# One fixed total of 832 GpSimd scatters, divided anew over the stages of an eight-stage graph network

## The reference

```python
edge_index = jnp.stack([src, dst])
x = x + _L0_gnn_ref(_layernorm(x), ..., src, dst)            # mean of neighbours
x = x + _L0_ffn_ref(_layernorm(x)[None], ...)[0]             # half of the nodes through an FFN
x = x + _L1_gnn_ref(_layernorm(x), ..., edge_attr_3, edge_index)   # attention over edges
x = x + _L1_ffn_ref(_layernorm(x)[None], ...)[0]             # 8 experts, top 1, capacity
x = x + _L2_gnn_ref(_layernorm(x), src, dst, edge_weight, ...)     # weighted sum over edges
x = x + _L2_ffn_ref(_layernorm(x)[None], ...)[0]             # 8 experts, top 2
x = x + _L3_gnn_ref(_layernorm(x), ..., edge_index)          # two GCN convolutions
x = x + _L3_ffn_ref(_layernorm(x)[None], ...)[0]             # 8 experts, top 1

def _L2_gnn_ref(x, edge_row, edge_col, edge_val, weight_l, bias_l, weight_r, bias_r):
    h = x @ weight_l
    agg = jax.ops.segment_sum(edge_val[:, None] * h[edge_col], edge_row, num_segments=N)
    return agg + bias_l + x @ weight_r + bias_r
```

## Time and profile before

| | us |
|---|---|
| median of 3 runs, without the profiler | 3591.89 |
| lowest and highest of these | 3591.84, 3598.81 |
| span of the profiled execution | 4271.3 |
| PE busy in it | 3169.9 |
| the 416 weight scatters, POOL busy | 463.5 |
| the 416 count scatters, POOL busy | 408.1 |

### The profile page before, as it was taken

How to read it: one execution, slowest core, us unless ns; L and a number is a source line. 1 busy time by engine, 2 the same in 40 slices (tenths; PEclk the granted TensorE clock), 3 DMA queues, 4 the chain that set the end, 5 groups by cost and what they waited for, 6 DMA issues and landing times. The chain is left out here.

```text
span 4271.3 us, 47439 instructions
## 1 busy us (share of the span) xinstructions
PE 3169.9 (74%) x14365; PEld 2194.5 (51%) x14365; DVE 1967.2 (46%) x4724; ACT 1137.9 (27%) x2521; POOL 2014.5 (47%) x2031
## 2 busy tenths in 40 slices
PE   4777777976888888459955886228975885998966
PEld 3565655854444445248843553114553553445856
DVE  5444446924666666899961342000024336023332
ACT  3444441221222222249931110000022221012310
POOL 5666664664555555675555553770035552000032
PEclk9888988987888988669977998558987997999978
DMA  5455452004766766248831225004313114452434
GB/s 176 159 160 160 160 159 94 1 13 142 197 198 192 202 186 199 68 151 271 281 117 63 93 65 197 23 15 136 128 45 128 52 52 141 151 198 86 152 125 137
DMA packets 281656, 563.05 MB, mean 132 GB/s; under 512 B 61793, under 2 KB 184101, under 8 KB 280774
## 3 DMA queue, kind: packets, MB, share of 16 engines
q1 hardware_dynamic: 200070, 404.27, 28.4%
q0 software_dynamic: 81344, 155.76, 13.4%
HBM read 381.99 MB, written 177.86 MB: 131 GB/s over the span
## 5 line engine op out<-in xcount | busy, mean ns | idle before, releaser
L1282 PE MATMUL bank<-layer_gnn_h_nodes,layer_gnn_s_onehot_t 128*128 x1664 | 547.9, 457 | 110.4 <-issue 73.5
L146 POOL DMA_INDIRECT edge_counts<-repeats,count_cell x416 | 408.1, 981 | 360.8 <-SPq L2872 226.5
L155 POOL DMA_INDIRECT edge_weights<-shares,share_cell x416 | 463.5, 1114 | 240.8 <-issue 91.9
L1234 POOL DMA_INDIRECT layer_gnn_s_rows<-gat_rows,src_cols x416 | 401.6, 965 | 355.2 <-DMA kept_rows<-layer_gnn_s_rows 211.3
L527 POOL DMA_INDIRECT layer_gnn_sum_rows<-xn_rows,src_cols x416 | 417.8, 1004 | 199.1 <-issue 110.8
L2841 PE MATMUL bank<-layer_gnn_b_weights,xn_nodes 128*128 128x391 f32 x768 | 300.7, 534 | 205.1 <-issue 173.3
L1282 PEld LDWEIGHTS bank<-layer_gnn_h_nodes,layer_gnn_s_onehot_t 128*128 128x128 f32 x1664 | 317.7, 212 | 208.8 <-issue 135.8
L2841 PEld LDWEIGHTS bank<-layer_gnn_b_weights,xn_nodes 128*128 128x128 f32 x768 | 155.5, 203 | 349.8 <-issue 225.1
L1292 ACT ACTIVATE layer_gnn_s_enc<-bank 128x256 f32<-128x256 f32 x416 | 154.7, 384 | 592.1 <-PE bank L1275 345.7
L590 PE MATMUL bank<-layer_gnn_sum_onehot,layer_gnn_sum_rows 128*128 128x256 f32 x832 | 296.8, 442 | 2.0 <-issue 1.8
L1311 DVE TENSOR_TENSOR layer_gnn_s_mix<-bank,layer_gnn_s_enc 128x256 f32<-128x256 f32 x416 | 176.0, 423 | 257.9 <-PE bank L1282 124.2
(11 more groups left out here) (645 smaller groups left out, 6077.7 us busy)
## 6 DMA issues: line engine op xcount, KB each, us to landing
kept_rows<-layer_gnn_s_rows SPq DMA_DIRECT2D x104, 512.0 KB
layer_gnn_w_rows<-kept_rows SPq DMA_DIRECT2D x104, 512.0 KB
edge_weights<-layer_gnn_sum_zeros SPq DMA_DIRECT2D x56, 800.0 KB
layer_gnn_gcn_sum_counts<-edge_counts SPq DMA_DIRECT2D x50, 896.0 KB
layer_gnn_b_weights<-edge_weights SPq DMA_DIRECT2D x56, 782.0 KB
layer_gnn_s_dst_across<-in_dst_row SPq DMA_DIRECT2D x104, 256.0 KB
edge_counts<-layer_gnn_w_no_edges SPq DMA_DIRECT2D x25, 896.0 KB
layer_ffn_e_w<-in_l1f_w SPq DMA_DIRECT2D x16, 1024.0 KB
```

The costliest lines, as they stand in the source:

```text
L146: nc.gpsimd.indirect_dma_start(g.counts, bass.IndirectOffsetOnAxis(ap=g.cell[:, t:t + 1].bitcast(U32), axis=0), g.repeats[:, t:t + 1], Non ...
L155: nc.gpsimd.indirect_dma_start(g.weights, bass.IndirectOffsetOnAxis(ap=g.share_cell[:, t:t + 1].bitcast(U32), axis=0), g.shares[:, t:t + 1 ...
L1234: nc.gpsimd.indirect_dma_start(rows[:, t % U, :], None, htable, bass.IndirectOffsetOnAxis(ap=g.srcc[:, t:t + 1].bitcast(U32), axis=0)).the ...
L1282: last = nc.tensor.matmul(g.ps[4 + t % 4][:, 0:D + HEADS], onehot_t[:, t % 4, k, :], hflat[:, ds(w * AW + (k * AW + HEADS), D + HEADS)], s ...
```

## The change

The two tables get other boundaries, `COUNTED` one entry more, and the count scatters of `weighted_products` a wait before each.

| stage | before | after |
|---|---|---|
| first FFN | 20 + 118 weights | the same |
| `gat_features` | 36 weights | 48 weights |
| `edge_softmax` | 36 weights | 50 weights |
| `weighted_sum`, on `summed` | 148 weights | 162 weights |
| gate of the second FFN | 16 weights | 18 weights |
| its route | 16 weights | 16 counts |
| its experts 0 and 1 | 13 weights + 12 counts each | 15, 16 counts |
| its experts 2 to 7 | 12, 12, 12, 12, 12, 13 counts | 15, 16, 15, 16, 15, 16 counts |
| `weighted_products` | 205 counts in one run | 162 counts, each behind a wait on `used` |
| all later stages | 114 counts | the same |

```diff
+def place_counts_beside(nc, g, pool, lo, hi, signal, first, steps):
+
+    for t in range(lo, hi):
+        pool.wait_ge(signal, first + (t - lo) * steps // (hi - lo))
+        place_counts(nc, g, pool, t, t + 1)
...
-PLACED = (20, 138, 174, 210, 358, 374, 390)
-COUNTED = (97, 302, 336, 348, 374)
+PLACED = (20, 138, 186, 236, 398, 416)
+COUNTED = (16, 140, 302, 336, 348, 374)
...
-        route(nc, g, "sw_route", logits, 1, CAP, SLOTS, r, g.xn, table, lambda pool: place_weights(nc, g, pool, PLACED[5], PLACED[6]))
+        route(nc, g, "sw_route", logits, 1, CAP, SLOTS, r, g.xn, table, lambda pool: place_counts(nc, g, pool, 0, COUNTED[0]))
...
-                first_of = lambda e: COUNTED[0] * e // E
-                left_of = lambda e: PLACED[6] + (ET - PLACED[6]) * min(e, 2) // 2
+                first_of = lambda e: COUNTED[0] + (COUNTED[1] - COUNTED[0]) * e // E
...
-                    place_weights(nc, g, pool, left_of(e), left_of(e + 1))
...
-            place_counts(nc, g, pool, COUNTED[0], COUNTED[1])
+            place_counts_beside(nc, g, pool, COUNTED[1], COUNTED[2], used, 4, len(order) - 6)
...
-            place_counts(nc, g, pool, COUNTED[1], COUNTED[2])
+            place_counts(nc, g, pool, COUNTED[2], COUNTED[3])
```

8 lines of the change are left out of this document (4 added, 4 removed).

## The result

| | us |
|---|---|
| kernel before, median of 4 runs | 3591.86 (3589.09 to 3598.81) |
| changed kernel, median of 4 runs | 3626.49 (3625.73 to 3629.37) |
| ratio, 95% interval | 1.0094 (1.0082 to 1.0106) |
| forecast | 3611.0, range 3545 to 3630 |

The changed kernel is slower, by 34.6 us, where the forecast had +19. Its profile is of another kind than the one of the kernel before. The page first: span, busy time, and the granted clock in 40 slices.

A forecast was written before the change was run, and what follows sets the result against it. No engine is near full, so each stage is decided by its own slowest engine. For runs without the freeze, 3591.9 + 13 (front) + 6 (softmax), other terms 0, gave 3610.9 us, 0.53% slower; range 3545 to 3630, the forecast's own 3600 to 3620.

The forecast's parts named there:

- the freeze: Three profile stretches, together 312 us, where PE almost stands still while POOL issues scatters one behind the other.
- front: Attention front, 36 to 48 scatters: POOL and DVE end level, 15.2 us stand out less 2 us cover: +13.
- softmax: Edge softmax, 36 to 50 scatters: the added 17.8 us outlast POOL's 12.2 us idle by 5.6: +6, bounds 0 and 7.
- `weighted_sum`: 148 to 162 scatters: 206 us of POOL beside 299 us, paced by `summed` as before: 0.
- gate: Second FFN's gate, 16 to 18 scatters: 2.5 us fit in the 6.98 us before the next block: 0, at most 2.5.
- experts: Second FFN's experts, 123 to 124 scatters: POOL's 29.8 us per expert hidden by PE's 30.3: 0, at most 3.
- product with waits: Product, 205 to 162 scatters with waits: scatters already hidden, last four still end ahead: 0, at most +5.
- Whether the timed runs freeze: Question the prediction turns on; answered no by PE-work sums, most of the freeze belonging to the recording of the profile.
- Rival 1: Timed runs freeze as the profile does; pacing the product gives back 215 us, other stages cost 25: 3402 us; chance 0.14.
- The signs that I named: Changed profile: no slow product passes, product some 215 us sooner, span near 4081 us, while the time goes up.
- Rival 2: The 0.30 us between POOL instructions are the profiler's, a scatter costs 0.96 us: 3596 us, within 0.2%; chance 0.21.
- Rival 3: Added softmax scatters take 2.7 us each, as most before them: 3631 us; chance 0.05.

The follow-up runs named there:

- frozen: Condition of a batch in which the unchanged kernel before took 4276 to 4305 us, in all its runs alike.
- quiet: Condition of a batch in which the unchanged kernel before took about 3595 us.
- Batches A and D: Quiet. A: kernel before unchanged (3594.56 us) and one stage changed at a time; D: scatters redistributed by slack, product waits added, against kernel before, 3579.35 us, ratio 0.9966.
- batches B, C and E: Frozen, against kernel before. B: changed kernel again, two variants, scatters redistributed by slack; C: that redistribution again, kernel before with waits (0.9558); E: second redistribution with waits (0.9554).
- batch B: Frozen; changed kernel run again unedited, 4085.86 us against 4275.65 for the kernel before, ratio 0.9558.
- the softmax alone: Kernel before with only the edge softmax raised from 36 to 50 weight scatters, product 191 instead of 205: 3597.40 us, ratio 1.0006.
- three single changes: Each against kernel before: front 36 to 48 scatters, ratio 1.0022; softmax 36 to 50, 1.0006; second FFN's experts evened to 15 or 16, 1.0006.
- the first profile: First recorded profile of the unchanged kernel before, which the prediction read: span 4271.3 us, against a timed median of 3591.86 us.

## Why the prediction was right, and where it was not

**The sign and the mechanism were right.** The time was taken without the freeze; POOL's scatters end the front and the softmax; the frozen product hid a product whose passes PE alone bounds. The working on PE foretold 2982 us of PE work for a kernel without the freeze, and the quiet profile has 2977.7. **The size was not.** The change costs 34.6 us, not 19. That lies in the range of 3545 to 3630, which was drawn wide for the rivals, but outside the forecast's own 3600 to 3620. Softmax, experts and product each came out beyond the bounds set for them, and the product's −4.6 took back a part of what the others missed. That the batch which was timed was a quiet one was luck, as shown below. The quiet pair of profiles gives for each term:

| term | forecast | stage in the quiet profiles |
|---|---|---|
| front | +13 (4 to 15) | +14.2 |
| softmax | +6 (0 to 7) | +10.0 |
| `weighted_sum` | 0 | +2.5 |
| gate | 0 (to 2.5) | +2.2 |
| route | 0 | −0.7 |
| experts | 0 (to 3) | +8.7 |
| product with waits | 0 (to +5) | −4.6 |
| sum | +19 | +32.3, timed +34.6 |

*Front.* I set DVE's undisturbed end by the evictions' 1.14 us 3 us ahead of POOL. It is 12.9 us ahead. The 3.9 us from there to the next stage I counted from the last eviction's start; from its end it is 3.4. The 2 us of cover that I took off were not there.

*Softmax.* The working was sound nearly to the last step. POOL ended 12.0 us ahead of DVE, as read from the earlier trace rows, and now ends 7.6 behind, 19.5 us for 14 scatters (forecast 17.8). What I left out is that a stage which a scatter ends is followed 3 us later than one that DVE ends. I compared neither nor the earlier trace rows, whose stages both end in DVE's work, with a stage that ends in a scatter.

*Experts.* This is the step that failed outright. "Both kernels hide it" rested on PE's 242.6/8 = 30.3 us from a frozen window. Undisturbed it is 27.8 us from one expert to the next, less than POOL's 29.8 by my own count, so POOL bounds the loop. And I added up what an expert costs without asking when POOL's inputs are there: the early surplus of 25 scatters was useful work in a wait. The +8.7 is the profile's; in time it was not confirmed, as said above.

*`weighted_sum`.* 1.27 us a scatter was taken from the front. Here 161 steps take 1869.88 − 1596.66 = 273.2 us, 1.70 each, in the changed kernel, 41 us of it idle for landings and 33 for the pairs. The last ends 0.9 us ahead of DVE, where the 148 ended 9.9 us ahead, and the barrier opens behind POOL.

*Product.* "Already hidden, so that taking 43 away gains nothing" was nearly so: POOL ended 4.4 us ahead of PE, but its `DRAIN` ended 3.4 us behind PE, whose next pass came 3.7 us behind its last (2486.15), for 0.84 in the changed kernel. Taking scatters away gave 4.6. My bound reached only upward.

Softmax, `weighted_sum` and product have one cause in common: POOL's `DRAIN` behind the last scatter lies on the way to the barrier, and a cover that looks like 1 to 5 us is none. The experts have a cause of their own, the order.

**Whether the timed runs freeze.** The answer for these times was right, by the sums that I made. The reason behind it was not. I held the freeze to be the recording's. Batches A and D have profiles without it, and batches B, C and E have it in all of their runs, not only in the one shown as a profile. So the passage on the Trainium skill's page "NOTIFIC — the notification-queue block", section 7.1, does not explain it: the page states what a full record path does to an engine, and no run here shows one. With the freeze in the timed runs and a profile of the same kernel without it (3592.8 us beside 4271.3), the recording alone is not the cause. Rival 1, which had 0.14, is not wrong but true under another condition. It said that pacing gives back 215 us and the rest costs 25, a profile of 4081 us; in batch B the profile is 4076.3 and the time falls by 190. So this change is −4.4% or +0.9%, depending on the condition of the machine in which it is timed, and nothing in the kernel decides which.

**The signs that I named.** I wrote that the product would have no slow passes: so it is. That the span would be 4081 while the time goes up held only in a frozen batch, with a time that goes down there. Rival 2 (the 0.30 us gaps are the profiler's, within 7 us of 3592) is refuted by 3626.5. Rival 3 (2.7 us for each scatter in the softmax) is refuted by the rows and by the softmax alone.

**Open.** The three single changes as timed give, by their ratios, +8, +2 and +2 us. Two of them hold the product's gain of 5, which the changed kernel has once, so 5 is added, and 2.5 + 2.2 from the profiles: about +22, not 34.6. The lengths of the stages in the profiles of the same kernels do add up (15.9 + 8.7 + 8.1 with the same 4.7, less 5, is 32), but their spans, 8.3, 2.4 and 7.4 us above the kernel before's 3592.8, give 28 with the same additions. The intervals of each are some 6 us wide, which may be all; I cannot show that it is. Nor is it known what makes a batch frozen. Batches B and D carry the same chip number, one frozen and one quiet, so it is not simply the chip.

## What to carry to other kernels

Before reading costs from a profile, set its span beside the median of the times, and where they are 19% apart get another profile before anything else: a stage's slack read in a disturbed profile (PE's 30.3 us per expert for 27.8) turns the bound around. Work that is hidden on an idle engine is hidden only if it ends ahead of the others by what the barrier takes after it (here 3 to 8 us), and moving it later in a loop can cost too. Where one engine's work may disturb another's, try a wait on the disturbed engine's progress: here it cost nearly nothing (product and sums 355.3 us with it, 354.8 without) and took away most of the harm.

## What the runs showed of the hardware

- **The freeze belongs to stages in which POOL issues many indirect DMAs.** The last two stretches of the program are the same in a frozen profile (332 and 364 us) and a quiet one (334 and 364), with DMA shares of 0.40 and 0.42 in both. They hold 64 such DMAs. The first gathers, with 416, take 659 for 579 us, the attention gathers and softmax 856 for 669, the experts 351 for 272.
- **It grows with the number of unbroken scatters.** Beside the product the passes take 218 us too long with 205, 214 with 198 and 168 with 162 scatters: 1.04 to 1.08 us for each. PE's first slow pass comes 34 to 40 us behind the first of them, and the granted clock falls to 0.51, near the lower level of 1.2 GHz, while PE has 57.76 us of work in 189.
- **PE's signals and the loads suffer before its passes do.** In the first profile PE is at full speed until 2657, but the piece that ends at 2644.06 has no event of `used` before 2648.28, and the DMA share falls from 0.54 (2628 to 2638) to 0.29 (2638 to 2648), where a quiet profile keeps 0.51. SP loads a piece only when `used` tells it to.
- **A wait on PE's progress keeps it short** at the same number of scatters: 331 instead of 516 us for 896 passes with 205, and 298 in a quiet profile.
- **Behind a scatter the barrier takes longer, by POOL's `DRAIN`.** The next stage starts 3.9, 4.9, 4.4 and 5.6 us after the end of POOL's last scatter where that is last or nearly so, where DVE is last it is 1.4 to 1.6 us after DVE's end in the softmax and `weighted_sum`, and 3.4 in the front, which still stores what DVE evicted. The `DRAIN` ends 3.0 to 4.3 us behind the last scatter in these stages, and 6.7 to 7.8 us behind it beside the product with 191 to 205 scatters; with 162, which have pauses between them, it is 4.3 there too.
- **A scatter's pace depends on the stage:** 1.27 us from one to the next in the front, 1.70 beside `weighted_sum`, where the DMA share is 0.8 and POOL idles 41 us for landings and 33 us on the wait for the pairs.
